# Powers of a charge: product before the transpose, or after it

## The chip, the cores and the metric

The kernel runs on one core of one Trainium2 chip. The metric is device time in microseconds for one execution, the median of three runs. Engines are named TensorE (PE in the profile; PEld is its weight load), VectorE (DVE), ScalarE (ACT), GpSimd (POOL) and SyncE (SP, which here only issues DMAs). Each has its own queue, taken in order.

## What is computed

`x` is (32, 512, 256) in float32: 32 sequences of 512 tokens. Attention with an explicit feature map is added to it, then a routed slot layer:

```python
def block(x):
    # both on layernorm(x); d1 adds to x, then d2 adds to the new x
    # d1, attention
    q = tanh(x @ W_charge.T + b_charge)[..., 0]              # one number per token
    phi_c = mags * q[..., None] ** arange(5)                  # 1, q, q^2, q^3, q^4
    shell = x @ W_shell.T + b_shell                           # 64 wide
    shell = shell / max(norm(shell), 1e-12)
    proj = shell @ omega.T + rff_bias                         # 32 angles
    phi_s = concat([cos(proj), sin(proj)]) * rff_scale        # 64
    phi = (phi_c[..., :, None] * phi_s[..., None, :]).reshape(b, n, 320) @ W_combine.T   # 64
    attn = softmax(causal(phi @ phi.T * decay / temp))
    d1 = (attn @ (x @ W_v.T + b_v)) @ W_out.T + b_out
    # d2, slots
    route_logits = (gelu(ctx @ w1.T + b1) @ w2.T + b2) / (|tau| + 0.1)        # 64 slots
    topk_vals, topk_idx = top_k(route_logits, 8)
    alpha = softmax(topk_vals) scattered to 64
    slot_input = alpha.T @ x, divided by its weight sum
    S_new = gru(slot_input, slots)
    d2 = (alpha @ (S_new @ wv.T + bv)) @ wo.T + bo
```

## The kernel before

Sequences go in pairs, 16 of them. A pair has d = 0, 1, and each sequence has four tiles of 128 tokens. The tile work is software pipelined over four stages by hand. Every engine has one loop, `for it in range(NP + 3)`, and in a pass of it works on four pairs at once: `f = it` (norm, projections, features, the score operands), `m = it - 1` (the causal softmax and its product with the values, eight row blocks n = 0 to 7), `g = it - 2` (routing, top eight, gather) and `o = it - 3` (slot update, output, store). `@live` drops a step whose pair doesn't exist. Passes 0 and 1 have no g, passes 16 to 18 no f. The order inside an engine's pass is the order written in its loop; nothing reorders it. Semaphores (one per step, counted up) are the only links between engines.

PSUM has eight banks in three rings: `T` (three banks) for transposes, `L` (two) for the scores, `G` (three) for the rest. `Ring.take` gives the next bank and a wait for whoever emptied it last.

The path of the features of pair f in a pass:

- TensorE `xn_t` (transposes of the normed input) and `proj` (L252: 354 columns, values, the 64 of the shell, the charge, 32 angles, in a split of high and low parts). VectorE `vs` (L749) adds the bias into `VS`.
- GpSimd `square`, VectorE `norm_sum`, GpSimd `rnorm` (a power of -0.5) for the shell's norm.
- VectorE `phase` (L766, L770: the angle for sine and again, a quarter turn on, for cosine), `turns`, `unwind` (L785, L788) and `clamp` (L794): range reduction over both halves, 512 elements a partition. `row_max(m, 3)` and `new_slots(o)` follow `unwind`; `clamp` comes after `al_low(o)`.
- ScalarE `charge` (L575, the tanh into `qq`, 8 elements) and `sine` (L583, into row 0 of `tp`).
- GpSimd `powers` (L1109, L1111: q^2, q^3, q^4, tiny) and `feats` (L1120, one per sequence: `tp` rows 1 to 4 are row 0 times the powers). Tokens are still on the partitions, so a power is a scalar of each partition and tile.
- TensorE `tp_t`: 24 transposes of `tp`, in six groups spread among the attention steps; ScalarE `feats_t` (L595) copies each group to `tpT`, which lies in `xmT` and `tpT2`. TensorE `phi` (L279): six matmuls of 512 columns.
- VectorE `qk_full`, ScalarE `qk_high`, GpSimd `qk_low`, SP `qk_moves` build the operands of the next pass's `logits`.

The attention steps of pair m: TensorE `logits` (L295, L297, L299), VectorE `row_max` (L809), ScalarE `expo` (L613, into `E`), TensorE `e_t` (L228, transposes), ScalarE `probs_t` (L623, into `ET`), TensorE `values` (L322), VectorE `attended` (L822).

The routing steps of pair g: TensorE `hidden` (L347), ScalarE `gelu` (L643), TensorE `route` (L359), VectorE `top` (the eight greatest, and `match_replace`, which writes the logits with those eight replaced by a very negative number to `lg[:, d, 1]`), GpSimd `shift` (L1136, subtracts the greatest, from both halves of `lg`), ScalarE `route_exp` (L649, both halves), GpSimd `pick` (L1144, the difference leaves the eight), VectorE `weight_sum` (L861), GpSimd `alpha` (L1154), TensorE `gather` (L373).

The slot steps of pair o that matter here: TensorE `gx_n`, `al_t`, `slot_v` (L430), `out_mm` (L445); ScalarE `al_high` (L675), `sv_high` (L680); VectorE `candidate`, `new_slots` (L903, L908); GpSimd `slot_change` (L1160) and `sv_low` (L1166); SP `alpha_moves` and `slot_moves`.

GpSimd's `norm` (L1059 to L1068) turns mean and variance into a scaled, shifted row for both layer norms, four times a pass.

The loop of GpSimd in one pass before: `square` x2, `rnorm`, `powers`, `slot_change(o)`, `feats` x2, `sv_low(o)`, `shift(g)` x2, `pick(g)` x2, `ln_norm`, `alpha(g)` x2, `lm_norm`, `ln_norm`, `qk_low(f)`, `lm_norm`.

## Time and profile before

| | |
|---|---|
| median of three runs | 843.04 us (842.33 to 845.62) |
| the profiled execution | 842.98 us |
| its span in the trace | 841.2 us |
| TensorE busy | 759.1 us, 90% |
| VectorE busy | 624.9 us, 74% |
| GpSimd busy | 514.3 us, 61% |
| ScalarE busy | 414.0 us, 49% |

The profile is of one execution of 842.98 us, near the median, so times of the trace can be set against it directly. In the steady state passes repeat every 47.3 us. A row of a timeline gives the start, the time until the last of the merged instructions ended, the line and operation, output and input with sizes, the count, and in brackets the engine's idle time just before and whose event ended it.

### The profile page before, as it was taken

What the parts mean: (1) busy time and instruction counts of PE and PEld (TensorE: products, weight loads), DVE (VectorE), ACT (ScalarE), POOL (GpSimd) and SP (SyncE); (2) the same over time, 40 slices, a digit from 0 to 9 for tenths busy, and PEclk for the clock granted to TensorE, in tenths of its full rate; (3) what the DMA queues carried; (4) which work ended last, traced back from release to release, by engine and by line L of the source; (5) the groups of instructions that cost most, each with busy time, mean ns of one, the idle gap of its engine ahead of it and who ended that gap; (6) DMA issues with size and microseconds to landing.
All of it is one profiled execution on the core that took longest, in us unless ns stands there. A gap on an engine that the chain in (4) does not pass through costs nothing.

```text
span 841.2 us, 15464 instructions
## 1 busy us (share of the span) xinstructions
PE 759.1 (90%) x4704; PEld 609.2 (72%) x4704; DVE 624.9 (74%) x2054; ACT 414.0 (49%) x886; POOL 514.3 (61%) x873
## 2 busy tenths in 40 slices
...
GB/s 280 3 6 120 39 88 39 112 66 138 51 176 51 125 92 61 149 63 142 51 174 53 125 93 66 144 65 138 52 175 51 119 97 68 94 61 132 60 99 101
DMA packets 69785, 80.33 MB, mean 96 GB/s; under 512 B 9990, under 2 KB 52552, under 8 KB 69704
## 3 DMA queue, kind: packets, MB, share of 16 engines
...
q14 instruction: 42, 0.34, 0.1%
...
## 4 chain that ended last, share of the span: by engine, by line
PE 64%; DVE 13%; POOL 10%; issue 5%; SPq 3%; ACT 3%; DMA 2%; DVEq 0%; POOLq 0%; ACTq 0%
PE ps L322 14%; PE ps L252 14%; PE ps L228 11%; PE ps L279 5%; PE ps L388 3%; PE ps L373 3%; POOL n L1103 3%; PE ps L359 3%; PE ps L445 2%; DVE xl L738 2%; PE ps L446 2%; PE ps L430 2%; DVE tg L766 2%; POOL xn L1068 2%; DVE tg L770 1%
## 5 line engine op out<-in xcount | busy, mean ns | idle before, releaser
L322 PE MATMUL ps<-VS,ET 128*128 128x256 f32 x640 | 159.6, 384 | 4.9 <-ACT ET L623 4.8
L322 PEld LDWEIGHTS ps<-VS,ET 128*128 128x128 f32 x640 | 112.9, 190 | 28.4 <-issue 17.4
L1120 POOL TENSOR_TENSOR tp<-tp,qq 128x1024 f32<-128x1024 f32 x32 | 60.2, 1903 | 100.4 <-ACT tp L583 100.4
L749 DVE TENSOR_TENSOR VS<-ps,biasM 128x354 f32<-128x354 f32 x128 | 67.2, 525 | 49.6 <-PE ps L252 49.5
L634 ACT ACTIVATE xmT<-ps 128x512 f32<-128x512 f32 x64 | 35.9, 586 | 109.4 <-PE ps L228 99.1
L252 PE MATMUL ps<-W1h,xh 128*128 128x354 f32 x256 | 86.6, 338 | 0.1
L252 PE MATMUL ps<-W1l,xh 128*128 128x354 f32 x256 | 82.6, 323 | 0.0
L252 PE MATMUL ps<-W1h,xl 128*128 128x354 f32 x256 | 82.5, 322 | 0.0
L822 DVE SCALAR_TENSOR_TENSOR X<-ps,rinv,X 128x256 f32<-128x256 f32 x128 | 61.9, 484 | 25.0 <-PE ps L322 20.0
L1096 POOL TENSOR_TENSOR tg<-VS 128x256 f32<-128x256 f32 x32 | 19.6, 613 | 93.7 <-DVE VS L749 89.6
L567 ACT ACTIVATE xh<-ps 128x512 fp32r<-128x512 f32 x64 | 35.3, 598 | 82.4 <-PE ps L228 82.3
L1068 POOL TENSOR_SCALAR xm<-X,rs 128x256 f32<-128x256 f32 x128 | 69.4, 556 | 3.3
L1068 POOL TENSOR_SCALAR xn<-X,rs 128x256 f32<-128x256 f32 x128 | 69.3, 555 | 3.3
L1061 POOL TENSOR_TENSOR rs<-rs,half 128x4 f32<-128x4 f32 x64 | 66.1, 1033 | 5.3
L613 ACT ACTIVATE E<-ps,nmax 128x128 f32<-128x128 f32 (+3 forms) x128 | 67.2, 525 | 3.8 <-DVE nmax L809 3.4
L228 PE MATMUL ps<-ident,tp 128*128 128x128 f32 (+1 forms) x384 | 54.2, 281 | 12.1 <-POOL tp L1120 11.3
L809 DVE TENSOR_REDUCE nmax<-ps 128x1 f32<-128x128 f32 (+3 forms) x128 | 60.8, 476 | 5.4 <-PE ps L299 5.3
L228 PEld LDWEIGHTS ps<-ident,tp 128*128 128x128 f32 (+1 forms) x384 | 44.6, 134 | 21.8 <-issue 18.1
L295 PE MATMUL ps<-KH,QS 128*128 128x256 f32 (+2 forms) x128 | 55.0, 430 | 5.7 <-ACT E L613 3.5
L347 PE MATMUL ps<-xmT,w1a 128*128 128x512 f32 x128 | 58.6, 599 | 0.1
L623 ACT ACTIVATE ET<-ps 128x128 f32<-128x128 f32 (+3 forms) x128 | 55.0, 430 | 4.8 <-PE ps L228 3.7
L228 PE MATMUL ps<-ident,E 128*128 128x128 f32 x320 | 56.8, 276 | 0.1
...
## 6 DMA issues: line engine op xcount, KB each, us to landing
...
QS<-xmT SPq DMA_DIRECT2D x64, 128.0 KB, 2.3
KH<-xmT SPq DMA_DIRECT2D x64, 128.0 KB, 2.3
KL<-xmT SPq DMA_DIRECT2D x64, 128.0 KB, 2.4
AS<-grz SPq DMA_DIRECT2D x32, 128.0 KB, 2.3
AS<-aTl SPq DMA_DIRECT2D x32, 128.0 KB, 2.4
...
```

The costliest lines, as they stand in the source:

```text
L228: ins = e.transpose(p[0:m, j * 128:j * 128 + 128], block_in, ident[:, :])
L252: ins = e.matmul(p[:, 0:FEATS], x[:, d, c, t * 128:t * 128 + 128], w[:, c, :], start=j == 0, stop=j == 5)
L295: e.matmul(p[:, 0:wide], QS[:, d, i * 128:w], KH[:, d, 0:wide], start=True, stop=False, skip_group_check=True)
L322: ins = e.matmul(p[:, 0:D], ET[:, r % 2, j * 128:j * 128 + 128], VS[:, (2 * k + d) % 4, j, 0:256], start=j == 0, stop=j == i)
L347: ins = e.matmul(p[:, :], w1a[:, c, :], xmT[:, d, c, :], start=c == 0, stop=c == 1)
L613: e.activation(E[:, r % 3, 0:w], at["lg", r][:, 0:w], ACT.Exp, bias=nmax[:, r % 8:r % 8 + 1], accum_out=rsum[:, r % 8:r % 8 + 1]).then_inc ...
L749: e.tensor_tensor(VS[:, b % 4, t, :], at["vs", b, t][:, 0:FEATS], biasM[:, :], ALU.add).then_inc(s["vs"], 1)
L809: e.tensor_reduce(nmax[:, r % 8:r % 8 + 1], at["lg", r][:, 0:w], AX.X, ALU.max, negate=True).then_inc(s["nmax"], 1)
L822: e.scalar_tensor_tensor(X[:, b % NX, i, :], at["av", r][:, 0:D], rinv[:, r % 8:r % 8 + 1], X[:, b % NX, i, :], ALU.mult, ALU.add).then_in ...
L1061: e.tensor_tensor(r[:, d, 0, :], r[:, d, 1, :], half[:, 0:4], ALU.pow).then_inc(s[tag + "_r"], 1)
L1068: ins = e.tensor_scalar(dst[:, t, :], x[:, t, :], r[:, d, 0, t:t + 1], r[:, d, 2, t:t + 1], ALU.mult, ALU.add)
L1120: e.tensor_tensor(tp[:, d, :, 1:5, :], tp[:, d, :, 0:1, :].broadcast_to([128, 4, 4, 64]), qq[:, d, :, :].unsqueeze(3).broadcast_to([128, 4 ...
```

## The change

The powers of the charge are multiplied in after the transpose. The features are transposed once (64 sines and cosines of both sequences side by side fill the 128 partitions: `z_t`, four transposes), and so is the charge, repeated 64 times (`q_t`, four transposes, copied to `QB`). GpSimd then makes Z[1] to Z[4] in a chain of four products, each by `QB`. Since the matmuls of `phi` need a sequence's rows stacked in pairs of powers, SP moves Z[0] to Z[3] of each sequence into `xmT` with eight DMAs; Z[4] is read in place. The angles are reduced at half width and the cosine's half is made from the sine's at the end: quarter turn minus the absolute value, the quarter turn being the bias of the sine. Of the top eight, one exponential of the logits and one of the eight values are taken; VectorE masks the logits by a comparison with the replaced half. The norms take (x - mean) * r and so lose one step of their chain.

```diff
+            def q_t(k):
...
+                e.wait_ge(s["q1"], k + 1)
+                transposes(p, [QN[:, t, :, :].rearrange("p b r -> p (b r)") for t in range(4)]).then_inc(s["q_t"], 1)
...
+            @live
+            def z_t(k):
...
+                e.wait_ge(s["sin"], k + 1)
+                transposes(p, [PS[:, t, :, :].rearrange("p b r -> p (b r)") for t in range(4)]).then_inc(s["z_t"], 1)
...
                     e.wait_ge(*before)
-                e.wait_ge(s["tpT"], 6 * k + 6)
-                for j in range(3):
-                    w = 128 if j < 2 else 64
+                e.wait_ge(s["zm"], 4 * k + 4)
+                e.wait_ge(s["zs"], 128 * (k + 1))
+                for j in range(2):
                     for d in range(2):
-                        ins = e.matmul(p[64 * d:64 * d + C, :], wc[0:w, j, :], tpT(d, j)[0:w, :],
-                                       start=j == 0, stop=j == 2)
+                        e.matmul(p[own(d), :], wc[:, j, :], stacked(d, j), start=j == 0, stop=False)
+                for d in range(2):
+                    ins = e.matmul(p[own(d), :], wc[own(d), 2, :], Z[own(d), 4, :], start=False, stop=True)
                 ins.then_inc(s["phi"], 1)
...
                 logits(m, 2)
+                q_t(f)
                 e_t(m, 0)
...
                 route(g, 1)
+                z_t(f)
                 values(m, 1)
-                if it == 0:
-                    e.wait_ge(s["soft"], SOFT)
-                tp_t(f, 0, 0)
                 logits(m, 5)
                 e_t(m, 3); values(m, 2)
-                tp_t(f, 0, 1)
                 logits(m, 6)
                 e_t(m, 4); values(m, 3)
                 logits(m, 7)
                 e_t(m, 5)
-                tp_t(f, 0, 2); tp_t(f, 1, 0); tp_t(f, 1, 1)
                 values(m, 4)
                 e_t(m, 6); values(m, 5)
-                tp_t(f, 1, 2)
                 e_t(m, 7)
+                if it == 0:
+                    e.wait_ge(s["soft"], SOFT)
                 phi(f)
...
-                e.activation(qq[:, :, :, 0:1], VP[:, :, :, 320:321], ACT.Tanh).then_inc(s["q1"], 1)
+                    e.wait_ge(s["z_t"], k)
+                VP = VS[:, (2 * k) % 4:(2 * k) % 4 + 2, :, 320:321]
+                e.activation(QN[:, :, :, :], VP.rearrange("p b t a -> p t b a").broadcast_to([128, 4, 2, 64]),
+                             ACT.Tanh).then_inc(s["q1"], 1)
+
+            @live
+            def q_copy(k):
+                e.wait_ge(s["q_t"], k + 1)
+                if k:
+                    e.wait_ge(s["zm"], 4 * k)
+                e.activation(QB[:, :], at["q", k][:, :], ACT.Copy).then_inc(s["qb"], 1)
...
+                e.wait_ge(s["q_t"], k + 1)
+                to = PS[:, :, :, :].rearrange("p t b r -> p b t r")
+
+                e.activation(to[:, :, :, 0:R], tg[:, :, :, 0:R], ACT.Sin, bias=quarter[:, 0:1])
+                e.activation(to[:, :, :, R:2 * R], tg[:, :, :, R:2 * R], ACT.Sin).then_inc(s["sin"], 1)
...
+                e.activation(Z[:, 0, :], at["z", k][:, :], ACT.Copy).then_inc(s["zc"], 1)
...
                 b = 2 * k + d
+                e.wait_ge(s["dm8"], b + 1)
+                e.activation(m8s[:, d, :, :], m8s[:, d, :, :], ACT.Exp).then_inc(s["ex"], 1)
                 e.wait_ge(s["dm"], b + 1)
-                e.activation(lg[:, d, :, :, :], lg[:, d, :, :, :], ACT.Exp).then_inc(s["ex"], 1)
+                e.activation(lg[:, d, 0, :, :], lg[:, d, 0, :, :], ACT.Exp).then_inc(s["ex"], 1)
...
-                expo(m, 1); probs_t(m, 0)
+                expo(m, 1); q_copy(f); probs_t(m, 0)
...
                 probs_t(m, 2)
-                feats_t(f, 0, 0)
+                z_copy(f)
                 expo(m, 4); probs_t(m, 3)
-                feats_t(f, 0, 1)
                 expo(m, 5)
                 route_exp(g, 0); route_exp(g, 1)
                 probs_t(m, 4); expo(m, 6); probs_t(m, 5)
-                feats_t(f, 0, 2); feats_t(f, 1, 0); feats_t(f, 1, 1)
                 expo(m, 7); probs_t(m, 6)
-                feats_t(f, 1, 2)
                 probs_t(m, 7)
...
+                i = (2 * k) % 4
+                e.tensor_tensor(ang[:, :, :, :], VS[:, i:i + 2, :, 321:353],
+                                n2[:, :, 0, :].unsqueeze(3).broadcast_to([128, 2, 4, R]),
+                                ALU.mult).then_inc(s["p1"], 1)
+                e.wait_ge(s["p1"], k + 1)
+                e.tensor_tensor(rows(ang), rows(ang), biasS[:, :].unsqueeze(1).broadcast_to([128, 8, R]),
+                                ALU.add).then_inc(s["p2"], 1)
...
-                e.wait_ge(s["p3"], 4 * k + 4)
-                e.tensor_scalar(angles(tg), angles(tg), PI_CLAMP, -PI_CLAMP, ALU.min, ALU.max).then_inc(s["trig"], 1)
+
+                e.wait_ge(s["p3"], 5 * k + 4)
+                e.tensor_scalar(rows(tg)[:, :, R:2 * R], rows(ang), PI_CLAMP, -PI_CLAMP, ALU.min,
+                                ALU.max).then_inc(s["p3"], 1)
+                e.wait_ge(s["p3"], 5 * k + 5)
+                e.scalar_tensor_tensor(rows(tg)[:, :, 0:R], rows(tg)[:, :, R:2 * R], -1.0, rows(tg)[:, :, R:2 * R],
+                                       ALU.mult, ALU.min).then_inc(s["trig"], 1)
...
-                e.wait_ge(s["am0"], b + 1)
-                e.tensor_reduce(asum[:, d, 0, :], lg[:, d, 0, :, :], AX.X, ALU.add).then_inc(s["as0"], 1)
+                e.wait_ge(s["ex"], 2 * b + 1)
+                e.tensor_reduce(asum[:, d, 0, :], m8s[:, d, :, :], AX.X, ALU.add).then_inc(s["as0"], 1)
+                e.wait_ge(s["ex"], 2 * b + 2)
+
+                e.scalar_tensor_tensor(lg[:, d, 0, :, :], lg[:, d, 1, :, :], -1e38, lg[:, d, 0, :, :], ALU.is_lt,
+                                       ALU.mult).then_inc(s["mk"], 1)
...
-                e.tensor_scalar(r[:, d, 1, :], m[:, d, :, 1], 1e-5, None, ALU.add).then_inc(s[tag + "_v"], 1)
+                e.tensor_scalar(r[:, d, 0, :], m[:, d, :, 1], 1e-5, None, ALU.add).then_inc(s[tag + "_v"], 1)
+                e.tensor_scalar(r[:, d, 2, :], m[:, d, :, 0], -1.0, None, ALU.mult).then_inc(s[tag + "_m"], 1)
                 e.wait_ge(s[tag + "_v"], b + 1)
-                e.tensor_tensor(r[:, d, 0, :], r[:, d, 1, :], half[:, 0:4], ALU.pow).then_inc(s[tag + "_r"], 1)
+                e.tensor_tensor(r[:, d, 1, :], r[:, d, 0, :], half[:, 0:4], ALU.pow).then_inc(s[tag + "_r"], 1)
+                e.wait_ge(s[tag + "_m"], b + 1)
                 e.wait_ge(s[tag + "_r"], b + 1)
-                e.tensor_tensor(r[:, d, 1, :], m[:, d, :, 0], r[:, d, 0, :], ALU.mult).then_inc(s[tag + "_m"], 1)
-                e.wait_ge(s[tag + "_m"], b + 1)
-                e.tensor_scalar(r[:, d, 2, :], r[:, d, 1, :], -1.0, None, ALU.mult).then_inc(s[tag + "_m2"], 1)
-                e.wait_ge(s[tag + "_m2"], b + 1)
                 for t in range(4):
-                    ins = e.tensor_scalar(dst[:, t, :], x[:, t, :], r[:, d, 0, t:t + 1], r[:, d, 2, t:t + 1],
-                                          ALU.mult, ALU.add)
+                    ins = e.tensor_scalar(dst[:, t, :], x[:, t, :], r[:, d, 2, t:t + 1], r[:, d, 1, t:t + 1],
+                                          ALU.add, ALU.mult)
...
-                e.tensor_tensor(tp[:, d, :, 1:5, :], tp[:, d, :, 0:1, :].broadcast_to([128, 4, 4, 64]),
-                                qq[:, d, :, :].unsqueeze(3).broadcast_to([128, 4, 4, 64]),
-                                ALU.mult).then_inc(s["tp"], 1)
+
+                e.wait_ge(s["zc"], k + 1)
+                e.wait_ge(s["qb"], k + 1)
+                for i in range(4):
+                    e.tensor_tensor(Z[:, i + 1, :], Z[:, i, :], QB[:, :], ALU.mult).then_inc(s["zm"], 1)
+                    if i < 3:
+                        e.wait_ge(s["zm"], 4 * k + i + 1)
...
                 b = 2 * k + d
                 e.wait_ge(s["mr"], 4 * b + 4)
-                for z in range(2):
-                    ins = e.tensor_tensor(lg[:, d, z, :, :], lg[:, d, z, :, :],
-                                          m8[:, d, :, 0:1].broadcast_to([128, 4, S]), ALU.subtract)
-                ins.then_inc(s["dm"], 1)
-
-            @live
-            def pick(k, d):
-                b = 2 * k + d
-                e.wait_ge(s["ex"], b + 1)
-                e.tensor_tensor(lg[:, d, 0, :, :], lg[:, d, 0, :, :], lg[:, d, 1, :, :],
-                                ALU.subtract).then_inc(s["am0"], 1)
+                e.tensor_tensor(lg[:, d, 0, :, :], lg[:, d, 0, :, :],
+                                m8[:, d, :, 0:1].broadcast_to([128, 4, S]), ALU.subtract).then_inc(s["dm"], 1)
+                e.wait_ge(s["dm"], b + 1)
+                e.tensor_tensor(m8s[:, d, :, :], m8[:, d, :, :], m8[:, d, :, 0:1].broadcast_to([128, 4, 8]),
+                                ALU.subtract).then_inc(s["dm8"], 1)
...
                 square(f, 0); square(f, 1)
-                rnorm(f); powers(f)
+                rnorm(f)
                 slot_change(o)
-                feats(f, 0); feats(f, 1)
+                powers(f)
                 sv_low(o)
                 shift(g, 0); shift(g, 1)
...
+            @live
+            def z_moves(k):
+
+                if k >= 2:
+                    e.wait_ge(s["h_mm"], 2 * (k - 2) + 2)
+                e.wait_ge(s["zc"], k + 1)
+                for i in range(4):
+                    if i:
+                        e.wait_ge(s["zm"], 4 * k + i)
+                    for d in range(2):
+                        e.dma_start(stacked(d, i // 2)[own(i % 2), :], Z[own(d), i, :]).then_inc(s["zs"], 16)
...
+
+            @live
+            def slot_rest_moves(k):
                 e.wait_ge(s["SVl"], k + 1)
...
+                z_moves(it)
+                slot_rest_moves(o)
```

GpSimd's queue, from the slot change of pair o to the end of the top-eight work of pair g, before (L1120 is `feats`, L1166 `sv_low`, L1136 `shift`, L1144 `pick`):

```order
L1160 TENSOR_TENSOR gt<-S,gn 128x256 [waits s_nn]
L1120 TENSOR_TENSOR tp<-tp,qq 128x4x256 [waits s_q4,s_sin]
L1120 TENSOR_TENSOR tp<-tp,qq 128x4x256
L1166 TENSOR_TENSOR gt<-gt,gn 128x256 [waits s_SVh]
L1136 TENSOR_TENSOR lg<-lg,m 128x256 [waits s_mr]
L1136 TENSOR_TENSOR lg<-lg,m 128x256
L1136 TENSOR_TENSOR lg<-lg,m 128x256 [waits s_mr]
L1136 TENSOR_TENSOR lg<-lg,m 128x256
L1144 TENSOR_TENSOR lg<-lg 128x256 [waits s_ex] x2
```

and with the change (L1132 is the new `powers`, L1174 `sv_low`, L1148 and L1151 `shift`):

```order
L1168 TENSOR_TENSOR gt<-S,gn 128x256 [waits s_nn]
L1132 TENSOR_TENSOR Z<-Z,QB 128x512 [waits s_qb,s_zc]
L1132 TENSOR_TENSOR Z<-Z,QB 128x512 [waits s_zm] x3
L1174 TENSOR_TENSOR gt<-gt,gn 128x256 [waits s_SVh]
L1148 TENSOR_TENSOR lg<-lg,m 128x256 [waits s_mr]
L1151 TENSOR_TENSOR m8s<-m 128x32 [waits s_dm]
L1148 TENSOR_TENSOR lg<-lg,m 128x256 [waits s_mr]
L1151 TENSOR_TENSOR m8s<-m 128x32 [waits s_dm]
```

Four dependent products over Z and `QB` stand where two over `tp` stood, they wait for ScalarE's copies (`zc`, `qb`) instead of the sine, and `sv_low` and the shifts stand behind them. The picks are gone.

ScalarE's queue, from the first copy of the features to the second softmax copy behind the routing exponentials, before (L595 `feats_t`, L613 `expo`, L623 `probs_t`, L649 `route_exp`):

```order
L595 ACTIVATE xmT<-ps 128x512 [waits s_qk,s_h_mm,s_phi,s_tpT_t]
L613 ACTIVATE E,rsum<-ps,nmax 128x128 [waits s_rinv,s_ET_t,s_nmax]
L623 ACTIVATE ET<-ps 128x512 [waits s_av_mm,s_ET_t]
L595 ACTIVATE xmT<-ps 128x512 [waits s_tpT_t]
L613 ACTIVATE E,rsum<-ps,nmax 128x256 [waits s_rinv,s_ET_t,s_nmax]
L649 ACTIVATE lg<-lg 128x512 [waits s_dm] x2
L623 ACTIVATE ET<-ps 128x128 [waits s_av_mm,s_ET_t]
L613 ACTIVATE E,rsum<-ps,nmax 128x384 [waits s_rinv,s_ET_t,s_nmax]
```

and with the change (L612 `z_copy`, L630 `expo`, L640 `probs_t`, L666 and L668 `route_exp`):

```order
L612 ACTIVATE Z<-ps 128x512 [waits s_qk,s_z_t]
L630 ACTIVATE E,rsum<-ps,nmax 128x128 [waits s_rinv,s_ET_t,s_nmax]
L640 ACTIVATE ET<-ps 128x512 [waits s_av_mm,s_ET_t]
L630 ACTIVATE E,rsum<-ps,nmax 128x256 [waits s_rinv,s_ET_t,s_nmax]
L666 ACTIVATE m8s<-m8s 128x32 [waits s_dm8]
L668 ACTIVATE lg<-lg 128x256 [waits s_dm]
L666 ACTIVATE m8s<-m8s 128x32 [waits s_dm8]
L668 ACTIVATE lg<-lg 128x256 [waits s_dm]
L640 ACTIVATE ET<-ps 128x128 [waits s_av_mm,s_ET_t]
L630 ACTIVATE E,rsum<-ps,nmax 128x384 [waits s_rinv,s_ET_t,s_nmax]
L640 ACTIVATE ET<-ps 128x256 [waits s_av_mm,s_ET_t]
```

One copy takes the place of two at this point, and ahead of the two `probs_t` of pair m there are now four exponentials, the first of each two waiting for the second product of a `shift`.

SP's queue between the alphas of pair o and the score moves of pair f, before (`SVS` and `SVL` are the slot values, high and low):

```order
L1300 DMA SVS<-gn 64x256 [waits s_SVh]
L1300 DMA SVS<-gn 64x256 x3
L1304 DMA SVL<-gt 64x256 [waits s_SVl]
L1304 DMA SVL<-gt 64x256 x3
L1277 DMA QS<-xmT 64x512 [waits s_Kh,s_Qh,s_lg_mm]
L1277 DMA QS<-xmT 64x512
```

and with the change, up to the second of the four pairs of moves out of Z:

```order
L1320 DMA SVS<-gn 64x256 [waits s_SVh]
L1320 DMA SVS<-gn 64x256 x3
L1286 DMA xmT<-Z 64x512 [waits s_zc,s_h_mm]
L1286 DMA xmT<-Z 64x512
L1286 DMA xmT<-Z 64x512 [waits s_zm]
L1286 DMA xmT<-Z 64x512
```

The moves from Z to `xmT` are new; two more pairs follow, each behind one more product, and then the moves to `SVL`, which stood directly behind `SVS` before.

## Rows read from the trace of the kernel before

**Rows 1.** The page's first part: busy us, share, instructions.

```profile
PE 759.1 (90%) x4704; PEld 609.2 (72%) x4704; DVE 624.9 (74%) x2054; ACT 414.0 (49%) x886; POOL 514.3 (61%) x873
```

**Rows 2.** One steady pass: length, busy us (count) by engine, clock, DMA.

```profile
447.30:494.60 47.30, 45.62 (x292) 36.81 (x291) 38.38 (x127) 25.34 (x56) 31.61 (x52) 1.00 0.39 101
```

**Rows 3.** Timeline of TensorE in one steady pass, and `phi` six passes later.

```profile
440.12 0.44 PE L295 MATMUL ps<-KH,QS 128*128 128x384 f32 x1 [0.20 <-ACT E L613]
...
443.07 3.65 PE L347 MATMUL ps<-xmT,w1a 128*128 128x512 f32 x8
...
448.50 1.10 PE L430 MATMUL ps<-Wvo,SN 128*128 128x256 f32 x4 [0.39 <-DVE SN L908]
...
451.45 1.08 PE L322 MATMUL ps<-VS,ET 128*128 128x256 f32 x4
...
452.98 0.36 PE L295 MATMUL ps<-KH,QS 128*128 128x256 f32 x1
...
458.58 1.47 PE L228 MATMUL ps<-ident,tp 128*64 128x128 f32 x12
459.89 0.60 PE L322 MATMUL ps<-VS,ET 128*128 128x256 f32 x2
...
462.88 1.94 PE L279 MATMUL ps<-xmT,wc 128*64 128x512 f32 x8 [0.34 <-ACT tpT L595]
...
746.71 1.94 PE L279 MATMUL ps<-xmT,wc 128*64 128x512 f32 x8 [0.34 <-ACT tpT L595]
```

**Rows 4.** Timeline of ScalarE in the same pass.

```profile
445.92 1.52 ACT L643 ACTIVATE hT<-ps,b 128x512 f32<-128x512 f32 x2
...
448.55 1.28 ACT L583 ACT_TABLE_LOAD   x1
449.84 0.63 ACT L583 ACTIVATE tp<-tg 128x512 f32<-128x512 f32 x1
...
453.41 0.59 ACT L595 ACTIVATE xmT<-ps 128x512 f32<-128x512 f32 x1
...
456.69 1.29 ACT L649 ACTIVATE lg<-lg 128x512 f32<-128x512 f32 x2
457.89 0.26 ACT L623 ACTIVATE ET<-ps 128x128 f32<-128x128 f32 x1
```

**Rows 5.** Timeline of GpSimd in the same pass.

```profile
450.55 3.76 POOL L1120 TENSOR_TENSOR tp<-tp,qq 128x1024 f32<-128x1024 f32 x2 [6.56 <-ACT tp L583]
454.27 0.73 POOL L1166 TENSOR_TENSOR gt<-gt,gn 128x256 fp32r<-128x256 f32 x1
454.95 2.36 POOL L1136 TENSOR_TENSOR lg<-lg,m 128x256 f32<-128x256 f32 x4
```

**Rows 6.** Groups by line: busy us, mean ns of one | idle before, releaser.

```profile
L1127 POOL TENSOR_TENSOR xmT<-xmT 128x512 fp32r<-128x512 f32 x16 | 20.5, 1279 | 0.7 <-ACT xmT L600 0.7
...
L1063 POOL TENSOR_TENSOR rs<-mv,rs 128x4 f32<-128x4 f32 x64 | 12.9, 201 | 5.0
...
L785 DVE SCALAR_TENSOR_TENSOR tg<-tg 128x512 f32<-128x512 f32 x16 | 11.1, 692 | 0.5
...
L575 ACT ACTIVATE qq<-VS 128x8 f32<-128x8 f32 x16 | 3.5, 220 | 37.9 <-DVE VS L749 37.9
```

**Rows 7.** VectorE writing `tg`: ns minimum/median/maximum, first, last start.

```profile
L766 DVE TENSOR_TENSOR tg<-VS,n x32: 282/295/826, 44.2 to 727.1; 128x128 f32<-128x128 f32 x32
```

**Rows 8.** Timeline of SP's queue in the same pass.

```profile
453.16 2.38 SPq L1300 DMA_DIRECT2D SVS<-gn  x4
```

**Rows 9.** The page's DMA issues: count, KB each, us to landing.

```profile
QS<-xmT SPq DMA_DIRECT2D x64, 128.0 KB, 2.3
```

**Rows 10.** Timeline of TensorE in pass 1.

```profile
81.07 1.56 PE L322 MATMUL ps<-VS,ET 128*128 128x256 f32 x4 [4.83 <-ACT ET L623]
```

**Rows 11.** TensorE in pass 1: length, busy us, granted clock, DMA.

```profile
80.00:84.00 4.00, 2.78 (x10) 0.70 0.00 0
84.00:88.00 4.00, 4.00 (x25) 0.88 0.00 0
```

More of the change, by code:

```diff
@@ L74 @@
 setup_mm setup_evac pool_setup soft ln_log slot_pool slot_chain slot_mm slot_evac
-ln_s ln_a ln_v ln_r ln_m ln_m2 ln_n lm_s lm_a lm_v lm_r lm_m lm_m2 lm_n
-xnT_t xnT xl vs_mm vs q1 sq n2 n2m rn q2 q4 p1 p2 p3 trig sin tp
-tpT_t tpT phi QF KF Qh Kh Ql Kl qk
+ln_s ln_a ln_v ln_r ln_m  ln_n lm_s lm_a lm_v lm_r lm_m  lm_n
+xnT_t xnT xl vs_mm vs  sq n2 n2m rn   p3 trig sin
+  phi QF KF Qh Kh Ql Kl qk
 lg_mm nmax E ET_t ET av_mm rinv av
-xmT_t xmT h_mm h rt_mm lg m8 mr dm ex am0 as0 as1 am gi_mm rw0 rw gin gi_t gi
+xmT_t xmT h_mm h rt_mm lg m8 mr dm ex  as0 as1 am gi_mm rw0 rw gin gi_t gi
 rz_mm grz srz gx_mm rhn gn nn hd hz sn aT_t aT aTl as sv_mm sv SVh SVl of_mm fin
+q1 q_t qb z_t zc zm zs
+p1 p2 sin2 dm8 mk
 """.split()
@@ L630, in xm_copy @@
                     later = min(k + 1, NP - 1)
-                    e.wait_ge(s["qk"], 192 * (later + 1))
+                    e.wait_ge(s["phi"], later + 1)
                     if k:
@@ L1198, in following @@
                     e.wait_ge(s["pool_setup"], n)
-                e.wait_ge(s["w"], 16 * 6)
-                for m in range(5):
-                    following(e.memset(wcs[64 * (m % 2):64 * (m % 2) + 64, m // 2:m // 2 + 1], MAGS[m] * RFF))
+                e.wait_ge(s["w"], 16 * 7)
+                for m in range(4):
+                    following(e.memset(wcs[own(m % 2), m // 2:m // 2 + 1], MAGS[m] * RFF))
+                following(e.memset(wcs[:, 2:3], MAGS[4] * RFF))
                 following(e.tensor_scalar(t8(0), ltb, -1.0, None, ALU.mult))
```

117 lines of the change are left out of this document (42 added, 75 removed).

## The prediction

> **What bounds the kernel now.** I read the page's first part [rows 1], then one pass of the loop in the steady state. TensorE is busy 90% of the span, and in a steady stretch of one pass 45.62 of 47.30 us [rows 2]. The first and last of the rows for `phi` in [rows 3] lie six passes apart: (746.71 - 462.88) / 6 = 47.3 us each. TensorE is the bound, with about 1.7 us idle in each pass. [Rows 3] show three of its holes: 0.20 us before `logits(m,2)` for ScalarE's `expo(m,0)`, 0.39 us before `slot_v` for VectorE, 0.34 us before `phi` for ScalarE's last copy. The others wait for `xl` and stay. Next I read ScalarE and GpSimd, since a transposed product puts new work there. In [rows 4] ScalarE takes `route_exp` at 456.69 without waiting, and directly behind it, at 457.89, `probs_t(m,4)`, on which TensorE's `values(m,4)` at 459.89 rests. `route_exp` needs GpSimd's `shift`, which runs 454.95 to 457.31 behind `feats` and `sv_low` [rows 5]. So GpSimd is off the path today by a margin of about 2 us, which the order of its queue sets.
>
> **TensorE's work.** 24 transposes a pass (`tp_t`) become 8 (`q_t`, `z_t`). Twelve take 459.89 - 458.58 = 1.31 us [rows 3], 0.11 each, so 16 fewer give back **1.75 us** a pass if nothing else is late. `phi` keeps its six matmuls of 512 columns. In the first half of a pass, though, TensorE gets later. `charge` writes 128x512 instead of 128x8: 0.63 us, as the sine, instead of 0.22 [rows 6]. It stands ahead of `expo(m,0)`, so the 0.20 us hole becomes 0.61. `q_t` adds 4 x 0.11 = 0.44. `hidden` then starts 0.85 later than in [rows 3], at 443.92, and ends at 447.4. I keep the clock of that pass from here on.
>
> **VectorE** gets shorter before `new_slots`: the angle steps halve from 512 to 256 elements, so the two of `unwind`, 692 ns each [rows 6], come near 420, and one addition goes. I estimate 1.3 to 1.9 us less, against 0.8 us more of waiting for `gx_n`. The 0.39 us hole goes; TensorE reaches `z_t` at 451.45 - 0.39 + 0.85 = 451.9. `clamp` becomes two steps, about 0.3 us more, ready at about 450.2. The mask in `weight_sum` adds two steps of 0.42, nearly paid by sums over 32 elements instead of 256; I cost both at nothing, as VectorE then waits for `phi`. Without that cover they cost 0.5 us a pass.
> In the diff two angle steps and the mask read two SBUF operands on VectorE while GpSimd may work. L766 of `phase` takes 282 ns at least and 826 at most for one and the same form [rows 7], so something holds part of its instances. The Trainium skill, GPSIMD Engine Reference, Key points, says that GpSimd contends with VectorE instructions of two SBUF inputs; the rows fit that, and by it each mask could take up to a GpSimd instruction longer.
>
> **ScalarE up to `z_copy`.** [Rows 4] again: the second `gelu` (two in 1.52) waits for `hidden`, so it runs from 447.5 to 448.25; the copy of `al_high` 0.6; the table load 1.28 to 450.15. VectorE's angles are there at 450.2. From the sine at 449.84 to the first feature copy at 453.41 the queue needs 3.57 us now; the same queue with two half sines needs 3.8, so `z_copy` starts at 454.1, takes the 0.59 of that copy and ends at **454.7**. The sines end at 451.1, before TensorE is at `z_t`, so no hole there. `expo(m,3)` is 0.7 later, and `logits(m,5)` loses 0.3 to it: it starts at 453.5.
>
> **GpSimd, the step that decides.** `powers` is now four dependent products of 128x512. Nearest row: L1127, the same size, two full operands, 1279 ns [rows 6]; back to back 1.25. Four and three handovers of 0.08: 5.25 us, from 454.7 to 460.0. In the old order `feats` took 3.76 but began at 450.55 [rows 5]. Behind `powers` stand `sv_low` (0.68 to 460.7) and the two `shift`, each one product of 0.59 and a small one, 0.3 with its handover (L1063: 201 ns, [rows 6]): to **462.45**, against 457.31 now. Dropped `pick` and the shorter norms (one small step of four each, 0.3 us) stand behind this and do not help.
> ScalarE waits at `route_exp` for it, with `probs_t(m,4)` queued behind. Exponentials to 463.05, `probs_t(m,4)` to 463.3, `values(m,4)` at **463.35**. TensorE is there at 451.9 + 0.44 + 0.87 for `z_t` and `values(m,1)` + 0.3, so 453.5 at `logits(m,5)`. From there to `values(m,4)` it needs 6.9 us now (452.98 to 459.89 in [rows 3]), of which 16 transposes were 1.75, so it arrives at 458.7: a new hole of **4.7 us**. After it the way to `phi` is 2.99 less four transposes (0.44) less the old hole of 0.34 plus 0.15 for a softmax that now comes just in time: `phi` at 465.7 instead of 462.88. **Plus 2.8 us a pass**, and nothing in the rest gives it back: GpSimd's later norms end some 2 us later than now, as TensorE does.
>
> **The DMAs.** `z_moves` issues eight moves on SP, 0.6 us each (four in 2.38, [rows 8]), landing 2.3 us after issue [rows 9], behind `slot_moves`. The first can go at 456.2, the last at about 460.3, landing at 462.6. In front of a `phi` at 465.7 this costs nothing; if the stall were away TensorE would be at `phi` at 461.1 and wait 1.5 us for them. `slot_rest_moves` goes behind: `SVL` lands by about 466.5, before `out_mm` at 471.6.
>
> **The clock.** After a wait of 4.83 us [rows 10] the granted clock fell to the lower level, 1.2 GHz: 0.70 and 0.88 in the two stretches from 80 to 88 us [rows 11], a loss of 0.30 x 4 + 0.12 x 4 = 1.68 us. My hole of 4.7 us is nearest to that row. I take 1.2 us a pass, since part of a fall can lie inside the hole and part in places where ScalarE is late anyway; bounds 0 and 1.68. The Trainium skill, TensorE: Matmul & The Clock Gate, Why this matters for your kernels, warns that an idle gap of TensorE between bursts of matmuls can bring the lower clock back; the row agrees.
>
> **The sum.** `powers` and `shift` meet in passes 2 to 15, 14 of them. 14 x 2.8 = 39.2; clock 14 x 1.2 = 16.8. Ends: pass 1 has no routing, and the 4.83 us wait [rows 10], for a softmax copy behind the sine and the long angle chain, shrinks by 1.2 us and the six copies go: -2.4 until GpSimd's norms hold it. Pass 0 pays +0.4 to +1, since `powers` and the landing are longer than `feats`. Together -2. On the profiled 842.98 (span 841.2), which is the median of 843.04 within 0.1: 842.98 + 39.2 + 16.8 - 2.0 = **897 us**.
>
> **Rivals.** (1) *The clock stays high.* Same stall, but 4.7 us of idle are less than the 4.83 that were followed by a fall. Against: only 0.1 us apart. It gives 880. By the page's rule it would not happen. (2) *The stall is hidden.* If ScalarE reached `z_copy` and GpSimd ended `shift` by about 458, TensorE would meet only the DMAs at `phi`: 462.6 for 462.88, no gain in the steady pass, 838 to 841 with the ends. For: GpSimd idles before 450.55 [rows 5]. Against: `z_copy` cannot come before 453.4, ScalarE's own queue. (3) *Faster.* TensorE gets its transposes back: -1.75, -0.39, -0.34, +0.41 and +0.1 = -2.0 a pass, 16 passes, 811. It decides at the same place: both the four products and the eight moves must fit into the 9.2 us from 451.9 to 461.1. Even at 0.6 us a product, half the row, `shift` would end near 459.8, and the hole would still be 2 us. So the products would have to be that fast and `z_copy` 2 us earlier; no row shows either. (4) *Worse*: VectorE, held at `weight_sum` until about 462, has then some 5 us of queue (two `attended`, the statistics of a tile pair, two masks) before `qk_full`, by my estimate 0.5 us to spare. If the masks and statistics contend, up to 1.5 us a pass more: above 913.
>
> **Chances.** Forecast 0.56, rival 1 0.24, rival 2 0.06, rival 3 0.05, rival 4 0.09. The low end of the range is the stall with `powers` at 1.0 us a product and no fall (+1.8 a pass): 866. The high end is +3.5 and 1.68 a pass: 913. Outside lie rivals 2, 3 and half of 4. Over 0.5% (4 us) is about what a measurement of this kernel can tell from no change: faster 0.06, same 0.04, slower 0.90.
>
> **What would show it.** Right: TensorE waits 4 to 5 us at the first matmul of `values(m,4)` for ScalarE's copy, ScalarE waits before the small exponentials for GpSimd, the four products take 1.25 us each, and the pass is 50 to 51.5 us; DMA is not named before `phi`. The clock columns show dips behind the hole in most passes. Wrong if `powers` takes much less than 5 us, if `z_copy` runs before 453, or if the wait of TensorE sits at `z_t` or `phi`.

## The result

| | before | after |
|---|---|---|
| median | 842.7 us (842.2 to 845.6, 4 runs) | **913.3 us** (912.8 to 913.8, 4 runs) |
| ratio, 95% interval | 1 | 1.083 (1.080 to 1.085) |
| span of the profiled execution | 841.2 us | 912.0 us |
| mean granted clock | 0.973 | 0.929 |
| steady pass | 47.30 us | 52.27 us |

The changed kernel is 8.3% slower. The forecast was 897 with a range of 866 to 913, and the measured time stands at the very end of it: the direction, the place and the mechanism were right, the size was 16 us short. In what follows a hole is a stretch in which TensorE is idle, and a fall is one in which its granted clock goes from 2.4 to 1.2 GHz (from 1.00 to 0.50 in the views). From the first part of the page of after, and its row of the granted clock in 40 slices:

```profile
PE 765.7 (84%) x4448; PEld 601.3 (66%) x4448; DVE 611.9 (67%) x2069; ACT 387.2 (42%) x870; POOL 484.0 (53%) x777
PEclk9869999989999998989999998999899899989986
```

Every engine has a smaller share than in [rows 1], and VectorE, ScalarE and GpSimd have less work in microseconds too, GpSimd by 30 us. Only TensorE's busy time is longer, 765.7 for 759.1, although it has 256 matmuls fewer (16 transposes in 16 passes): part of its work runs at the lower clock. So nothing got busier. Something waits. Which, the groups of waits of after say (engine and line, what it waited for: us in total, times, longest):

```profile
POOL Z L1132 <- ACT Z L612: 153.0, 16, 10.5
ACT m8s L666 <- POOL m8s L1151: 70.6, 30, 5.1
PE ps L337 <- ACT ET L640: 65.6, 14, 4.8
```

Read from the last row upwards. TensorE waits 14 times, once in each of the passes 2 to 15, up to 4.8 us at `values` (L337) for ScalarE's `probs_t`. ScalarE waits at `route_exp` (L666) for the small product of GpSimd's `shift`. GpSimd waits for `z_copy` (L612), and then runs its four products. The 153 us of GpSimd's own wait are not a cost; it has nothing to do then. One pass in time, first ScalarE, then GpSimd, SP's queue and TensorE, each from its timeline (start, duration, line and operation; in brackets the idle time before it and who ended it):

```profile
490.04 0.60 ACT L612 ACTIVATE Z<-ps 128x512 f32<-128x512 f32 x1
...
497.64 0.23 ACT L666 ACTIVATE m8s<-m8s 128x32 f32<-128x32 f32 x1 [4.20 <-POOL m8s L1151]
...
498.77 0.23 ACT L666 ACTIVATE m8s<-m8s 128x32 f32<-128x32 f32 x1 [0.59 <-POOL m8s L1151]
498.90 0.40 ACT L668 ACTIVATE lg<-lg 128x256 f32<-128x256 f32 x1
499.21 0.26 ACT L640 ACTIVATE ET<-ps 128x128 f32<-128x128 f32 x1
```

```profile
490.72 5.32 POOL L1132 TENSOR_TENSOR Z<-Z,QB 128x512 f32<-128x512 f32 x4 [9.89 <-ACT Z L612]
496.00 0.72 POOL L1174 TENSOR_TENSOR gt<-gt,gn 128x256 fp32r<-128x256 f32 x1
496.68 0.62 POOL L1148 TENSOR_TENSOR lg<-lg,m 128x256 f32<-128x256 f32 x1
...
498.27 0.47 POOL L1151 TENSOR_TENSOR m8s<-m 128x32 f32<-128x32 f32 x1
```

```profile
492.59 5.19 SPq L1286 DMA_DIRECT2D xmT<-Z  x8
```

```profile
499.61 1.19 PE L337 MATMUL ps<-VS,ET 128*128 128x256 f32 x2 [4.75 <-ACT ET L640]
...
503.94 2.83 PE L293 MATMUL ps<-xmT,wc 128*64 128x512 f32 x8
```

Four products, `sv_low`, two shifts, four exponentials, one copy: a chain with hardly a gap from 490.72 to 499.47, and TensorE at its end. `phi` at 503.94 has no wait: the last move of Z had been issued at 497.8 and takes 2.4 us to land. `phi` takes 2.83 us in this pass; in [rows 3] it takes 1.94. The same matmuls at another clock, as the windows of TensorE show (stretch: length, busy us, granted clock, DMA share and GB/s):

```profile
499.00:501.00 2.00, 1.39 (x4) 0.50 0.42 105
501.00:503.00 2.00, 2.00 (x8) 0.50 0.13 32
503.00:505.00 2.00, 2.00 (x9) 0.50 0.00 0
505.00:507.00 2.00, 2.00 (x10) 0.81 0.00 0
```

TensorE comes back from the hole at 1.2 GHz and stays there some 6 us. That is the part of the loss that I had too small.

### The profile page after: what moved, and what is told of

It is laid out like the page before. It is cut to its first block, busy times and chain, and to the rows that moved or that the text cites. A ratio compares the mean times of both kernels' runs of the same rounds, so it can differ in the third digit from the quotient of the medians.

```text
span 912.0 us, 15097 instructions
## 1 busy us (share of the span) xinstructions
PE 765.7 (84%) x4448; PEld 601.3 (66%) x4448; DVE 611.9 (67%) x2069; ACT 387.2 (42%) x870; POOL 484.0 (53%) x777
## 4 chain that ended last, share of the span: by engine, by line
PE 59%; POOL 15%; ACT 8%; issue 7%; DVE 7%; SPq 2%; DMA 1%; ACTq 0%; POOLq 0%; DVEq 0%
PE ps L260 14%; PE ps L337 10%; POOL Z L1132 9%; PE ps L236 8%; PE ps L362 6%; PE ps L403 4%; PE ps L293 4%; PE ps L388 3%; PE ps L460 2%; DVE xl L754 2%; POOL lg L1148 2%; PE ps L295 2%; PE ps L461 2%; ACT ET L640 1%; PE ps L310 1%
## 5 line engine op out<-in xcount | busy, mean ns | idle before, releaser
L337 PE MATMUL ps<-VS,ET 128*128 128x256 f32 x640 | 178.8, 417 | 65.6 <-ACT ET L640 65.6
L337 PEld LDWEIGHTS ps<-VS,ET 128*128 128x128 f32 x640 | 123.1, 208 | 93.9 <-issue 80.9
L1132 POOL TENSOR_TENSOR Z<-Z,QB 128x512 f32<-128x512 f32 x64 | 81.4, 1272 | 156.8 <-ACT Z L612 153.0
L765 DVE TENSOR_TENSOR VS<-ps,biasM 128x354 f32<-128x354 f32 x128 | 67.3, 525 | 51.2 <-PE ps L260 51.2
L630 ACT ACTIVATE E<-ps,nmax 128x128 f32<-128x128 f32 (+3 forms) x128 | 67.2, 525 | 23.0 <-DVE nmax L830 22.8
L1088 POOL TENSOR_SCALAR xn<-X,rs 128x256 f32<-128x256 f32 x128 | 71.4, 571 | 5.8 <-POOL rs L1084 5.8
L640 ACT ACTIVATE ET<-ps 128x128 f32<-128x128 f32 (+3 forms) x128 | 55.4, 433 | 38.0 <-PE ps L236 37.8
L236 PE MATMUL ps<-ident,E 128*128 128x128 f32 x320 | 66.0, 312 | 0.3
L754 DVE TENSOR_TENSOR xl<-ps,xh 128x512 fp32r<-128x512 f32 x64 | 41.5, 686 | 17.1 <-ACT xh L580 15.4
L236 PEld LDWEIGHTS ps<-ident,E 128*128 128x128 f32 x320 | 46.3, 168 | 9.6 <-issue 7.1
```

Source lines behind the costliest of these rows:

```text
L236: ins = e.transpose(p[0:m, j * 128:j * 128 + 128], block_in, ident[:, :])
L337: ins = e.matmul(p[:, 0:D], ET[:, r % 2, j * 128:j * 128 + 128], VS[:, (2 * k + d) % 4, j, 0:256], start=j == 0, stop=j == i)
L630: e.activation(E[:, r % 3, 0:w], at["lg", r][:, 0:w], ACT.Exp, bias=nmax[:, r % 8:r % 8 + 1], accum_out=rsum[:, r % 8:r % 8 + 1]).then_inc ...
L640: e.activation(ET[:, r % 2, 0:w], at["E", r][:, 0:w], ACT.Copy).then_inc(s["ET"], 1)
L765: e.tensor_tensor(VS[:, b % 4, t, :], at["vs", b, t][:, 0:FEATS], biasM[:, :], ALU.add).then_inc(s["vs"], 1)
L1088: ins = e.tensor_scalar(dst[:, t, :], x[:, t, :], r[:, d, 2, t:t + 1], r[:, d, 1, t:t + 1], ALU.add, ALU.mult)
```

## Experiments

All times are medians on the chip, beside runs of the kernel before, whose medians there were 843.8 to 845.2 us. "Pass" is the steady distance between two `phi` or two `values(m,4)`.

| kernel | time, us | ratio to before | pass, us |
|---|---|---|---|
| fill | 897.2 | 1.061 (1.059 to 1.063) | 50.2 or 51.8 |
| fill_more | 882.9 | 1.047 (1.045 to 1.050) | 50.2 |
| two_products | 860.5 | 1.020 (1.017 to 1.023) | 47.8 to 50.3 |
| shift_first | 876.4 | 1.037 (1.034 to 1.039) | 48.9 or 50.1 |
| exp_late | 869.9 | 1.029 (1.027 to 1.032) | 49.0 mean |
| phi_late | 870.6 | 1.032 (1.031 to 1.034) | 48.5 or 50.0 |
| rowmax_only | 896.7 | 1.060 (1.055 to 1.064) | 51.2 |
| reordered | 827.9 | 0.981 (0.980 to 0.983) | 45.9 |
| charge_late | 825.0 | 0.977 (0.975 to 0.980) | 45.7 |
| small_parts | 838.2 | 0.991 (0.990 to 0.993) | 47.0 |

### How much of it is the clock: work put into the hole

`fill`, and with ten instead of six `fill_more`:

```diff
+                if n == 4 and 2 <= k + 1 < NP:
+                    for _ in range(6):
+                        e.matmul(p[:, 0:D], ident[:, :], Wvo[:, 0, :], start=True, stop=True)
                 e.wait_ge(s["ET"], r + 1)
```

> The changed kernel, with six more matmuls of 256 columns (product discarded) on TensorE just before values(m,4) waits for its softmax copy, in passes 2 to 15. About 2.6 us of work inside the 4.75 us hole, which leaves 2.1 us idle. Theory (the hole costs 2.8 us a pass, the lower clock after it the rest, about 2.1 us): the clock stays at 1.00, the pass goes from 52.3 to 50.1 us, time 883 (878 to 890). Rival (the lower clock hides behind ScalarE, and the whole 5 us is the wait): 911 to 915.

Measured 897.2, between the two. The extra matmuls shorten the hole to 2.07 us but do not close it, and the clock still falls behind it in 7 of the 12 steady passes. Two neighbouring passes of `fill`, by their windows (length, then busy us of PE, PEld, DVE, ACT and POOL, then the clock):

```profile
236.83:287.05 50.22, 46.72 (x286) 37.18 (x287) 37.71 (x127) 23.57 (x55) 29.76 (x47) 1.00 0.46 116
287.05:338.87 51.82, 48.32 (x287) 38.33 (x287) 37.68 (x127) 23.67 (x55) 29.77 (x47) 0.97 0.45 112
```

The work of VectorE, ScalarE and GpSimd is the same in both, and the pass is 1.6 us longer where the clock fell. So the effect is real, but six matmuls weren't enough to take it away. I therefore filled the hole further.

> The changed kernel with ten extra matmuls of 256 columns (of a constant, overwritten after) before TensorE waits for values(m,4) in passes 2 to 15; the run with six of them left a hole of 2.07 us, after which the clock still fell in about every second pass. Its passes without a fall took 50.2 us, those of the changed kernel 52.27 on average. Theory (the stall costs 2.8 us a pass and the fall of the clock behind it about 2.1): the hole shrinks to 0.3 to 0.5 us, no pass has a fall, the pass is 50.1 to 50.3 us, the time 884 us (880 to 889). Rival (the clock falls from what stands before the hole, or the extra pass time is no clock matter): the time stays at 895 to 913 us.

Measured 882.9. The timeline of TensorE (the fill is the `Wvo,ident` row) and one pass:

```profile
482.20 4.48 PE L337 MATMUL ps<-Wvo,ident 128*128 128x256 f32 x20
487.05 0.70 PE L340 MATMUL ps<-VS,ET 128*128 128x256 f32 x2 [0.36 <-ACT ET L643]
```

```profile
388.99:439.22 50.23, 48.43 (x296) 38.67 (x295) 37.69 (x129) 23.59 (x54) 29.85 (x47) 1.00 0.46 116
```

This kernel has the whole stall and, in its steady passes, no fall. So the loss of after splits: the stall alone is 50.23 - 47.30 = **2.9 us a pass** (2.8 predicted), the clock 52.27 - 50.23 = **2.0 us a pass** (1.2 predicted). In whole times, 913.3 - 882.9 = 30 us of the 71 are the clock, nearly all of it in these 14 passes.

### Is it the chain of products: two of four made narrow

```diff
-                    e.tensor_tensor(Z[:, i + 1, :], Z[:, i, :], QB[:, :], ALU.mult).then_inc(s["zm"], 1)
+                    v = 8 if k >= 2 and i in (2, 3) else N
+                    e.tensor_tensor(Z[:, i + 1, 0:v], Z[:, i, 0:v], QB[:, 0:v], ALU.mult).then_inc(s["zm"], 1)
...
-                        e.dma_start(stacked(d, i // 2)[own(i % 2), :], Z[own(d), i, :]).then_inc(s["zs"], 16)
+                        e.dma_start(stacked(d, i // 2)[own(i % 2), :], Z[own(d), min(i, 2), :]).then_inc(s["zs"], 16)
```

This kernel leaves q^3 and q^4 out of the features; it serves only to price the chain.

> The changed kernel with the third and fourth product of powers only 8 columns wide from pass 2 on, and the last moves taking the second power's rows: q^3 and q^4 are left out of the features. The number of instructions, waits and DMAs stays. Theory (GpSimd's chain ahead of the shifts is the stall, 1.27 us a product): the shifts come 2.1 to 2.3 us earlier, TensorE's hole before values(m,4) is 2.5 to 2.7 us in place of 4.75; the clock falls in about half of the passes, as it did behind a hole of 2.07; pass 49.2 us, time 870 us (864 to 884, the upper end if it falls in each pass). Rival (the handovers and ScalarE's order make the stall, not the width): hole over 4 us, time over 900 us.

Measured 860.5 us. GpSimd's and TensorE's timelines:

```profile
465.51 3.19 POOL L1133 TENSOR_TENSOR Z<-Z,QB 128x512 f32<-128x512 f32 x4 [9.89 <-ACT Z L612]
```

```profile
617.72 0.67 PE L337 MATMUL ps<-VS,ET 128*128 128x256 f32 x2 [2.41 <-ACT ET L640]
665.56 0.67 PE L337 MATMUL ps<-VS,ET 128*128 128x256 f32 x2 [2.40 <-ACT ET L640]
```

The products take 3.19 instead of 5.32, 2.13 less, and the hole is 2.35 less. Between these two rows the pass is 47.84, which is the 50.23 above less those 2.35 (47.88): what the chain gives back the hole gives back, and the pass too, within 0.2 us. The clock fell in 4 of the 12 steady passes, less often than I had expected, so the time lies 3.5 us under the lower end of the theory.

### Taking the chain out of TensorE's way: two reorderings

`shift_first`, on GpSimd:

```diff
+                shift(g, 0); shift(g, 1)
                 powers(f)
                 sv_low(o)
-                shift(g, 0); shift(g, 1)
```

> The changed kernel with GpSimd's two shifts placed ahead of the four products. Theory (the hole comes from the order of GpSimd's queue): no wait before values(m,4); the products now end at about 462, the last move lands near 464, and TensorE waits some 2.7 us at phi instead, no or rare falls of the clock; 860 (854 to 868). Rival (four products and eight moves are simply too long for a pass wherever they stand): 900 or more.

Measured 876.4, 8 us above the theory's upper end. The hole at `values(m,4)` is gone, but `z_copy` ended at 374.5 in the pass shown, and the products start only at 377.05, since the second shift ahead of them waits for VectorE's `top(g,1)`. GpSimd's timeline, then TensorE's in the same pass:

```profile
376.15 0.62 POOL L1148 TENSOR_TENSOR lg<-lg,m 128x256 f32<-128x256 f32 x1 [2.13 <-DVE lg L876]
...
377.05 5.38 POOL L1132 TENSOR_TENSOR Z<-Z,QB 128x512 f32<-128x512 f32 x4
```

```profile
381.56 0.63 PE L236 MATMUL ps<-ident,E 128*128 128x128 f32 x4 [1.13 <-ACT E L630]
384.07 1.94 PE L293 MATMUL ps<-xmT,wc 128*64 128x512 f32 x8 [1.88 <-DMA xmT<-Z]
396.50 0.63 PE L236 MATMUL ps<-ident,xn 128*128 128x128 f32 x4 [1.41 <-POOL xn L1088]
```

Three waits stand where one was: for the last exponential of the softmax, for the moves of Z, and for GpSimd's second norm. My expectation had only the second.

`exp_late` leaves GpSimd alone. ScalarE takes `route_exp` behind `probs_t(m, 7)`, VectorE both `weight_sum` behind `attended(m, 5)`. ScalarE's part of the edit:

```diff
-                route_exp(g, 0); route_exp(g, 1)
                 probs_t(m, 4); expo(m, 6); probs_t(m, 5)
                 expo(m, 7); probs_t(m, 6)
                 probs_t(m, 7)
+                route_exp(g, 0); route_exp(g, 1)
```

> The changed kernel with ScalarE's four routing exponentials moved behind its last softmax copy, and VectorE's two weight_sum behind attended(m,5), since they would block it. Theory: ScalarE no longer waits for the shifts with a softmax copy queued behind; the wait of TensorE moves to phi, for the last move out of Z (lands 0.4 to 0.8 us later than phi stood before), about 2 us; time 852 (846 to 858). Rival (the exponentials are only the last in a row of waits behind GpSimd, and the next one costs as much): 890 or more.

Measured 869.9, again better than after by 43 us, and 12 us above the theory's upper end. The same three waits, in the same order: 1.15, 0.9 to 1.7 and up to 1.95 us. Both kernels show that the stall came from the order of the two queues, and that behind it other waits were ready.

### Which of the three waits sets the pass

I took them away in turn. (The "previous kernel" in the expectation of `reordered` is `phi_late`. `rowmax_only` came after both; it has one of the two steps that `reordered` adds.) `phi_late` is `exp_late` with `values(m, 6); values(m, 7)` ahead of `phi(f)` on TensorE, and both `attended` ahead of `qk_full` on VectorE.

> The kernel with the small exponentials late (869.9 us), and in addition TensorE does values(m,6) and values(m,7) before phi, VectorE attended(m,6) and attended(m,7) before qk_full. Its parent waits in a steady pass 0.9 to 1.7 us at phi for the last moves of Z, then 1.7 to 1.9 us for GpSimd's second norm xn. Theory (the pass is now set by a loop through GpSimd: xn, projections, angles, z_t, the four products, shift, norms, xn; the wait for the DMAs lies beside it): the hole at phi goes to 0 and the hole before xn_t grows by as much, time 866 to 872 us. Rival (the moves at phi set the pass): the hole before xn_t stays as it is and 1.0 to 1.2 us a pass are won, time 852 to 856 us.

Measured 870.6, the theory. `phi` no longer waits, and the time turns up at xn. Every steady pass has a row like this one:

```profile
491.45 0.63 PE L236 MATMUL ps<-ident,xn 128*128 128x128 f32 x4 [2.59 <-POOL xn L1088]
```

`rowmax_only` takes away the wait for the exponential as well, by moving one step on VectorE:

```diff
-                attended(m, 3); lm_stats(m, 2)
                 row_max(m, 7)
+                attended(m, 3); lm_stats(m, 2)
```

> phi_late (870.6 us, steady pass 48.46 us without a fall of the clock, 50.0 with one) and only row_max(m,7) before attended(m,3); GpSimd's norms stay in their old order. It takes away the hole of 1.15 us before e_t(m,7) and nothing else. Theory (the loop through GpSimd sets the pass): the hole before xn_t grows from 2.6 to about 3.7 us, the pass stays 48.4 to 48.6, time 866 to 876 us. Rival (holes on TensorE add up, each can be won by itself): the hole before xn_t stays 2.6, time 853 to 857 us.

Measured 896.7: 26 us **slower** than its parent `phi_late`, and 21 us above anything I had foreseen (one of its four runs took 888.2, the others 896.3 to 897.3). The hole before xn grew to 3.6 us, as the theory says. But the clock now falls in each pass. The windows of one pass of `phi_late` without and one with a fall, then one of `rowmax_only`:

```profile
480.55:529.01 48.46, 43.77 (x275) 34.80 (x274) 37.40 (x128) 23.47 (x54) 29.76 (x47) 1.00 0.48 121
529.01:578.99 49.98, 45.28 (x275) 36.30 (x275) 37.50 (x128) 23.47 (x54) 29.81 (x47) 0.97 0.47 116
```

```profile
493.71:544.90 51.19, 46.43 (x276) 37.46 (x275) 37.54 (x128) 23.69 (x54) 29.88 (x46) 0.93 0.46 116
```

The removed wait of 1.15 us and the one of 2.59 have become a single one:

```profile
505.65 1.09 PE L236 MATMUL ps<-ident,xn 128*128 128x128 f32 x4 [3.61 <-POOL xn L1088]
```

The sum is nearly the same; in one piece it costs 2.7 us a pass more than the pass without a fall. Since the loop through GpSimd closes over TensorE's projections, which run at the lower clock behind that hole, the fall lies on the loop itself: in `phi_late` the next hole before xn is 2.59 us after a pass with a fall as after one without, so that the slower work is not won back there.

`reordered` then breaks the loop. It is `phi_late` with the step of `rowmax_only`, and on GpSimd the second `ln_norm` and `qk_low` go ahead of both `lm_norm`.

```diff
                 alpha(g, 0); alpha(g, 1)
-                lm_norm(m, 0)
                 ln_norm(it + 1, 1)
                 qk_low(f)
+                lm_norm(m, 0)
                 lm_norm(m, 1)
```

> The previous kernel, and in addition GpSimd does the second ln_norm and qk_low before both lm_norm, and VectorE does row_max(m,7) before attended(m,3). Theory (loop through GpSimd): xn comes 3.7 us earlier, the hole before xn_t goes, the hole of 1.15 us before e_t(m,7) goes to 0.2 or less, the clock stays high, pass 45.2 to 46.0 us, time 820 us (813 to 828), below the kernel before. Rival (another wait takes its place: the score moves before logits, or GpSimd again): pass 47.3 or more, time 843 us or more.

Measured 827.9, at the theory's upper end, and 1.9% faster than before (1.7% to 2.1%). One pass:

```profile
455.95:501.89 45.94, 44.00 (x275) 34.78 (x274) 37.62 (x128) 23.68 (x54) 29.66 (x46) 1.00 0.52 129
```

TensorE is busy 44.00 us instead of 45.62 [rows 2]: this is where the 16 transposes, 1.75 by my count, are won at last. The chain on GpSimd is as long as ever,

```profile
492.32 5.34 POOL L1132 TENSOR_TENSOR Z<-Z,QB 128x512 f32<-128x512 f32 x4 [9.89 <-ACT Z L612]
```

only TensorE has no wait behind it any more.

`charge_late` asks for the price of the wider `charge`: `reordered` with `expo(m, 0)` ahead of it.

> reordered (827.9 us, pass 45.82) with ScalarE's charge behind expo(m,0) instead of ahead of it. My term for charge was 0.41 us a pass at logits(m,2); the hole there went from 0.20 to 0.52. Theory (charge on the path there): the hole goes back to 0.20 or goes away, -0.3 to -0.5 us in 16 passes, time 822 us (819 to 824). Rival (the time is given back at q_t or the following e_t): 827 to 829 us.

Measured 825.0 (822.7 to 826.9, against 826.5 to 828.7). The hole before `logits(m,2)` goes from 0.52 back to 0.20, the pass from 45.9 to 45.7: of the 0.32 us some 0.2 arrive. The time lies between theory and rival, and the two sets of runs overlap slightly. It is the fastest kernel here.

### The other three edits alone

`small_parts` is the kernel before with the shorter norms, the angles at half width and the one exponential with its mask; the powers stay as they were.

> The kernel before with three of the four parts: norms with one step less, angles at half width, one exponential for the top eight; the powers stay ahead of the transposes. Theory (the loss comes from the transposed powers alone): the 0.39 us hole before slot_v goes, ScalarE's two half sines cost 0.1 to 0.2; 837 (832 to 841). Rival (the masks and the second exponential cost as well): 846 or more.

Measured 838.2, 0.9% faster than before. The pass is 47.03: the 0.39 us hole before `slot_v` is gone, as my step on VectorE said, and 0.30 come back as a new one before a group of transposes. The masks and the second exponential, the rival, cost nothing that shows. So the loss of after is wholly the powers behind the transpose, or rather their place in two queues.

## Why the prediction was right or wrong

**TensorE's work, VectorE, ScalarE up to `z_copy`: right.** To compare, I shift the pass shown by 36.19 us, the distance of its first `logits` to that of [rows 3]. `z_copy` starts at 453.85 (454.1 predicted). The hole before `logits(m,2)` is 0.52 (0.61), that before `slot_v` is gone. The masks stayed off the path.

**GpSimd's chain: right.** Four products in 5.32 us (5.25), from 454.53 (454.7). `values(m,4)` at 463.42 (463.35), hole 4.75 us in 13 of 14 passes (4.7). The stall is 2.9 us a pass (2.8), and `two_products` shows it to be the chain's length.

**The DMAs: right.** In the passes with the stall they cost nothing, and 0.9 to 2.1 us once it is gone (1.5). Only the eight issues take 5.19 us, not the 4.8 of my 0.6 each.

**The clock: the term that was mis-sized.** I took 1.2 us a pass, "bounds 0 and 1.68", from the two 4 us stretches of [rows 11]. It was 2.0, above my upper bound. The step that failed is the reading of one fall as the most that a fall can cost; the steady passes of the kernel before have none (1.00 in [rows 2]), and a bound read from one instance should have been wider. The work behind that hole in pass 1 was back at 2.4 GHz within the second stretch. In the steady pass shown above it was 0.50 in three stretches of 2 us and 0.81 in the fourth: 0.50 x 6 + 0.19 x 2 = 3.4 us by the same sum, less 0.3 for the 0.61 us of it that lie in the hole. Three passes of after, each from one `values(m,4)` to the next, the last of them the one shown:

```profile
395.70:447.90 52.20, 46.02 (x274) 36.49 (x275) 37.62 (x127) 23.66 (x55) 29.76 (x47) 0.96 0.44 112
447.90:499.61 51.71, 45.55 (x274) 36.20 (x275) 37.64 (x127) 23.67 (x55) 29.75 (x47) 0.96 0.44 112
499.61:552.73 53.12, 46.94 (x275) 36.74 (x275) 37.64 (x127) 23.68 (x55) 29.78 (x47) 0.92 0.43 111
```

They are 2.0, 1.5 and 2.9 us longer than a pass without a fall, behind the same hole of 4.75 us, and the three lengths repeat in turn up to the last of these passes. Of the 16 us missing, 14 x 0.8 = 11 are this, and 1 to 2 the stall, which was 2.9 for 2.8.

**The ends: wrong, by some 4 us.** I had -2.0. TensorE's first `logits` of pass 2 start at 113.87 us for 111.36, already 2.5 late, and behind the last stall only 0.9 come back. In pass 1 the wait of 4.83 us became one of 3.46, now before `z_t` at 82.70; that it shrinks by 1.2 I had said. I also wrote "until GpSimd's norms hold it", but gave that no price. It has one, the second row below. Pass 0 I priced by the start of `phi` alone, which is right (56.58 for 56.38), and not by its clock. TensorE's timeline in passes 0 and 1 of after:

```profile
56.58 3.68 PE L293 MATMUL ps<-xmT,wc 128*64 128x512 f32 x8 [7.68 <-DMA xmT<-Z]
...
103.25 1.94 PE L236 MATMUL ps<-ident,xn 128*128 128x128 f32 x8 [3.03 <-POOL xn L1088]
```

The first 8 matmul records take 3.68 us instead of 1.94. Before the change 4.29 us of transposes stood just ahead of them, and the clock was at 1.00 from 56 to 58 us; now there is a wait of 7.68 us for the moves, and the clock is at 0.50. The wait in the second row was 0.76 us before the change.

**The range.** Its high end, 913, added a stall of 3.5 us a pass, which no row gave, to a fall of 1.68. The stall stayed 0.6 below that, the fall went 0.3 above and the ends 4 us; that the sum came out at 913.3 is luck. One of my signs of being right missed for the same reason: the pass is 52.27 us, not 50 to 51.5.

**The rivals.** Rival 1 (no fall, 880) is what `fill_more` looks like, 882.9, but after itself did not behave so: 4.75 us of idle were enough. For the clock the Trainium skill, TensorE: Matmul & The Clock Gate, Why this matters for your kernels, warns of idle gaps between bursts of matmuls. By that rule, which the traces bear out with a fall behind each hole of 4.75 us, this rival should have had less than its 0.24. The clock also fell behind shorter holes than the page warns of, such as those of 2.07 us in `fill`. Rivals 2 and 3 said what a kernel would do whose chain is hidden; I gave -2.0 us a pass for it, and `reordered` has 45.9 - 47.3 = -1.4. In the changed kernel as written neither had a chance. Rival 4 (VectorE held up) did not happen: in the pass shown VectorE waits 2.68 us for `phi` before `qk_full`. The time at its border came from the clock.
